# A tuned one-core attention and expert kernel: four of a quartet's sends issued ahead of GpSimd's next inverse deviations

## The reference

```
x = x + attention(layernorm(x), context, mask)     # 16 heads of 8, softmax, output weight Wo
h = layernorm(x)                                   # (v + 1e-5) ** -0.5
probs = softmax(h @ wg.T)                          # 8 experts
topk_w, topk_idx = top_k(probs, 2); topk_w /= sum(topk_w)
y[e] = (silu(h @ w1[e].T) * (h @ w3[e].T)) @ w2[e].T
x = x + sum over the two chosen e of topk_w * y[e]
```

## Time and profile before

| | |
|---|---|
| median of 3 runs | 311.91 us (311.3 to 312.0) |
| profiled execution, its own time | 308.16 us |
| its span | 306.4 us |
| mean granted TensorE clock | 0.893 |
| busy: PE, DVE, ACT, POOL | 75%, 72%, 46%, 37% of the span |
| chain that ended last, by engine | PE 44%, DVE 23%, DMA 14%, SP's queue 8%, issue 7%, ACT 2%, POOL 1% |
| POOL L989, sends | 24, mean 986 ns |
| POOL L972, waiting for DVE's variances (mv, L1059) | 67.6 us in 7 waits |

### The profile page before, as it was taken

The page is one execution under the profiler, slowest core; times in us unless marked ns, Lnnn a source line. Parts: engine busy times, 40 slices in busy tenths (PEclk is TensorE's granted clock), DMA queues, the critical chain, the costliest instruction groups (busy, mean ns, idle before and its releaser), DMA issues.

```text
span 306.4 us, 5812 instructions
## 1 busy us (share of the span) xinstructions
PE 230.8 (75%) x1591; PEld 179.1 (58%) x1591; DVE 219.5 (72%) x642; ACT 142.2 (46%) x318; POOL 114.1 (37%) x125
## 2 busy tenths in 40 slices
PE   0975788999899799695749772979598995999600
PEld 0752565666576566574537551768587994898500
DVE  5578976877578877977482762487788883789853
ACT  5785247554746375250244363435244552555200
POOL 5301250125011251053646343045266776354640
PEclk9996599999999999887586798699889998999955
DMA  6894522442244204427021151402112343254006
GB/s 188 251 275 99 116 49 61 89 99 65 48 101 86 43 19 98 91 63 206 12 52 35 30 111 42 116 9 65 51 51 71 92 111 96 63 137 128 29 21 194
DMA packets 43886, 27.31 MB, mean 89 GB/s; under 512 B 5030, under 2 KB 41397, under 8 KB 43856
## 3 DMA queue, kind: packets, MB, share of 16 engines
q1 hardware_dynamic: 40208, 20.95, 29.4%
q0 software_dynamic: 2816, 5.27, 5.6%
q10 hardware_dynamic: 832, 0.72, 0.9%
HBM read 13.27 MB, written 7.37 MB: 67 GB/s over the span
## 4 chain that ended last, share of the span: by engine, by line
PE 44%; DVE 23%; DMA 14%; SPq 8%; issue 7%; ACT 2%; POOL 1%; POOLq 0%; DVEq 0%
SPq L422 7%; PE bank L495 7%; DVE m_neg L1369 4%; DMA bd<-st 4%; DMA xg<-raw,rows_i 4%; PE bank L501 4%; PE bank L732 4%; PE bank L706 4%; PE bank L709 3%; PE bank L707 3%; PE bank L668 3%; PE bank L629 3%; PE bank L733 3%; PE bank L719 3%; PE bank L651 2%
## 5 line engine op out<-in xcount | busy, mean ns | idle before, releaser
L1028 POOL DMA_INDIRECT ys<-big x46 | 45.1, 981 | 36.0 <-DVE big L1392 14.4
L1369 DVE TENSOR_REDUCE m_neg<-bank 128x4 f32<-128x512 f32 x64 | 43.3, 682 | 15.3 <-PE bank L668 14.9
L909 ACT ACTIVATE big<-bank 128x512 f32<-128x512 f32 x64 | 37.5, 599 | 23.3 <-PE bank L654 22.8
L775 ACT ACTIVATE st<-bank 128x128 fp32r<-128x128 f32 (+1 forms) x92 | 26.3, 329 | 33.5 <-PE bank L719 19.4
L668 PE MATMUL bank<-bd,st 128*128 128x512 f32 x64 | 29.7, 496 | 5.9 <-DMA bd<-st 5.6
L989 POOL DMA_INDIRECT xg<-rows,rows_i x24 | 23.7, 986 | 26.8 <-DVE rows_i L1198 11.9
L651 PE MATMUL bank<-m_bd,ones_b 128*128 128x512 f32 x64 | 31.1, 486 | 2.6 <-ACT big L909 2.2
L1295 DVE SCALAR_TENSOR_TENSOR st<-st_hi,cst,bank 128x512 fp32r<-128x512 f32 x32 | 23.5, 747 | 9.3 <-ACT st_hi L775 4.6
L732 PE MATMUL bank<-bd,st 128*128 x92 | 27.3, 318 | 2.5 <-DVE big L1392 2.1
L941 ACT ACTIVATE big<-bank 128x256 f32<-128x256 f32 x46 | 17.7, 384 | 21.5 <-PE bank L709 20.2
L1411 DVE TENSOR_TENSOR big<-big,bank 128x256 f32<-128x256 f32 x46 | 19.2, 418 | 10.9 <-ACT big L941 10.5
(11 more groups left out here) (172 smaller groups left out, 560.9 us busy)
## 6 DMA issues: line engine op xcount, KB each, us to landing
bd<-st SPq DMA_DIRECT2D x128, 64.0 KB, 2.0
big<-xg SPq DMA_DIRECT2D x46, 64.5 KB, 1.9
raw<-ys SPq DMA_DIRECT2D x8, 256.0 KB, 4.0
xg<-in_patterns SPq DMA_DIRECT2D x18, 64.5 KB
x_all<-in_x SPq DMA_DIRECT2D x4, 256.0 KB, 4.3
rows<-in_mask_BxS_if POOLq DMA_DIRECT2D x4, 256.0 KB, 4.7
ctx_all<-in_L_ffn_w SPq DMA_DIRECT2D x1, 1024.0 KB, 6.4
out<-ctx_all SPq DMA_DIRECT2D x4, 256.0 KB, 3.6
```

What stands on the lines that cost most here:

```text
L775: return nc.scalar.activation(o, i, ACT.Copy)
L909: nc.scalar.activation(prob[n % 2][:, NJ * g:NJ * (g + 1), :].rearrange("p h q -> p (h q)"), s2[k % 2][:, :], ACT.Exp, scale=SCALE).then_i ...
L1028: pool.indirect_dma_start(ys[f], bass.IndirectOffsetOnAxis(xt[n % XR][:, D:RW].bitcast(I32), 0), y_sb[n % YR], None, bounds_check=2 * CAPS ...
L1369: nc.vector.tensor_reduce(m_neg[:, H * (b - 1) + NJ * g:H * (b - 1) + NJ * (g + 1)], s1[k % s1_ring(u)][:, :].rearrange("p (j q) -> p j q" ...
```

## The change

POOL's order alone is changed. The sends of quartet 1 are issued in two halves: batches 4 and 5 (four sends) right after the products of L1006 and ahead of the third quartet's inverse deviations, batches 6 and 7 after these.

```
-            def send_quartet(q):
+            def send_quartet(q, first, last):
                 pool.wait_ge(rows_ready, q + 1)
-                for m in range(2 * QB):
+                for m in range(2 * first, 2 * last):
                     send(QB * q + m // 2, m % 2)
...
                 if u + 1 == NQ:
                     inverse_deviation(NQ)
                     inverse_deviation(NQ + 1)
-                    send_quartet(0)
+                    send_quartet(0, 0, QB)
+            send_quartet(1, 0, 2)
             inverse_deviation(NQ + 2)
-            send_quartet(1)
-            send_quartet(2)
+            send_quartet(1, 2, QB)
+            send_quartet(2, 0, QB)
             inverse_deviation(NQ + 3)
```

## The result

| | before | changed kernel |
|---|---|---|
| median of 20 runs each, us | 311.96 (307.67 to 314.59) | 314.33 (310.31 to 317.67) |
| ratio, 95% interval | | 1.0093 (1.0052 to 1.0133) |
| profiled execution, own time, us | 308.16 | 314.76 |
| its span, us | 306.4 | 313.0 |
| mean granted clock | 0.893 | 0.875 |

The changed kernel is slower, by 0.93% or 2.9 us, with 1.6 to 4.1 us in the interval. The ratio leaves out executions in a slower state of the chip, so it is not the quotient of the two medians, which is 1.0076. Two later measurements of the same kernel, on other occasions, gave 1.0044 (0.9991 to 1.0097) and 1.0039 (1.0004 to 1.0073), 1.4 and 1.2 us. Single executions of one kernel are spread over some 7 us, so the total tells the sign and a size of 1 to 3 us. The mechanism has to be read from intervals inside the traces, which repeat far better.

What follows compares the result with a forecast made beforehand. One unbroken dependent chain, from DVE's third-quartet statistics to the first gathered tile, was taken as the bound. Delaying L1077 by 2.12 us, with nothing saved, gave 311.91 + 2.1 = 314.0 us, range 312.9 to 315.4.

Steps and rivals of the forecast that it cites:

- The sends don't fit into the gap: GpSimd's 3.49 us idle before L972 cannot hold four sends, since the third must wait until the first has landed.
- The sum for the delay: On GpSimd, four sends, then L972 and L973, put L1077 at 160.00 instead of 157.88: 2.12 us later.
- low bound of 1.7: Delay of L1077 in us with the low ends: 3.08 from first to third send, 0.03 for L972 behind a send.
- First send behind the products: On GpSimd, the first moved send starts 0.20 us after the products of L1006, at 152.86.
- first to third send: On GpSimd, 3.30 us, taken between 3.08 and 3.46 seen elsewhere, as no other transfer runs there.
- L972 behind a send: On GpSimd, the step from the fourth send's end to L972, taken as 0.20 us between bounds of 0.03 and 0.31.
- L972 to L973: On GpSimd, 0.31 us between these two instructions that make the inverse deviations.
- The slack of 0.34 us: Before L1077 on DVE, the inverse deviations could end 0.34 us later without delaying it.
- All steps to the first tile shift alike: Behind L1077, quartet 2's sends and SP's padding writes hang on DVE's routing, so the 2.1 us delay finds no cover.
- my first rival: TensorE's clock rises at the same moment though PE restarts later, giving 1.05 us back: +1.1, 313.0 us; chance 0.15.
- The expert stage starts from the gathered tile: In the expert stage every engine starts from the first gathered tile (189.61), so its delay carries through to the end.
- What the edit saves is worth nothing: Quartet 1's second half ends about 4 us sooner, but GpSimd already idled 4.02 us before quartet 2: worth 0.

Runs made afterwards that it cites:

- Warm_after: The changed kernel plus sixteen matmuls whose result nobody reads, on PE ahead of the turn of the third quartet's tokens; ratio 0.9962 to the kernel before.
- eight_ahead: The change with all eight sends of quartet 1, instead of four, ahead of the third quartet's inverse deviations; ratio 1.0258 to the kernel before.
- three_ahead: The change with three sends of quartet 1 instead of four ahead of the inverse deviations; 323.12 us in one execution, beside 323.06 for the kernel before.
- busy_ahead: The kernel before plus five unread powers on GpSimd between the products of L1006 and the inverse deviations, no send moved; ratio 1.0028.

## Why the prediction was right

The forecast was +2.1 us, 314.0 us, slower with 0.87; measured 314.33 us, and a ratio of 1.0093 where 1.0067 was forecast, which lies in all three intervals. The sign and the mechanism up to the token tags are right. That the median came within 0.3 us of the forecast is partly luck: the traces show 1.8 us at the tags but only 0.6 to 1.0 at the row numbers, and later measurements gave 1.4 and 1.2 us. The noise was also taken too small, 0.2%; the intervals reach 0.3 to 0.5% to either side. Step by step:

- **The sends don't fit into the gap.** Right. L972 has no wait for DVE left and starts as soon as the fourth send ends. With two sends the cost is zero, with three 0.55 us, with four 1.77, with eight 8.67.
- **The sum for the delay** was 2.12 us, measured 1.77, near the low bound of 1.7. First send behind the products 0.20, measured 0.16; first to third send 3.30, measured 159.65 - 156.50 = 3.15, so it lay nearer to the undisturbed 3.08 than to the 3.30 that I took; L972 behind a send 0.20, measured 0.02, the step for which there was no row and whose low bound was the right one; L972 to L973 0.31, measured 0.35. The landing for which the third send waits, that of the first, took 2.36 us on the chain. The Trainium skill ("DMA: Bandwidth & Descriptors", "Anatomy of one DMA — SWDGE (gpsimd) path") would have it 2.15 by its formula, an estimate, and the delay at 1.8. That is what came out, but through the 0.02 us and not through the landing, which was 0.21 longer.
- **The slack of 0.34 us** was right: with three sends the inverse deviations end 9.77 us behind the start of the products instead of 8.87, so 0.90 later, and the tags move by 0.55; 0.35 are absorbed.
- **"All steps to the first tile shift alike"** is the step that failed in size. Row numbers came 0.6 to 1.0 us late, not 1.8 or 2.1. Most of that was my first rival, given 0.15, by which the clock rises at the same moment though PE restarts later, and gives half of the shift back. It happened in all three profiled executions: the rise is 17.5, 17.1 and 16.8 us behind the start of the products, in the two of before 17.2 and 17.0. What I held against it, that the wait is longer and not shorter, was no argument, since the low stretch begins within the wait. The other 0.2 us are L1175's, which no rival named. Warm_after shows that nothing else up to the row numbers has slack.
- **"The expert stage starts from the gathered tile"** was right as far as eight_ahead tells: 7.73 us at the gather, 8.0 at the end.
- **What the edit saves is worth nothing.** Right for the sends: quartet 1 is sent 4.35 us sooner, and GpSimd's idle time ahead of quartet 2 grows to 9.26 us. But L1175 on DVE, which no longer meets the last of these sends, is 0.2 us shorter.

The delay less what comes back makes 0.8 us at the row numbers on average (24.89 over three executions of the change, 24.11 over two of before). The first gathers are on average 1.5 us later (42.04 and 40.49), and the totals 1.2 to 2.9 us. That the first measurement is above the two later ones is within their intervals; what it has beyond the 0.8 us is not explained by any run here, and the scatter of quartet 2's sends (15.0 to 16.7 us to the gather) is large enough to hold it.

## What to carry to other kernels

An idle gap on a side engine is room for other work only up to the moment at which the waited-for value arrives; count the moved instructions with their own waits against that gap, and look for who needs the result behind it. Here the gap held two sends and not four, and what was gained by sending early had no taker but for 0.2 us on DVE. Where a small change must be judged under a noise of its own size, make the same change larger (eight sends) and read intervals from a common instruction inside the trace.

## What was not expected of the hardware

- The low clock after PE's restart was shorter after the longer wait: 5.4 to 5.6 us after a wait of 4.2 (the tags-to-logits stretch 8.9 to 9.0 us in three executions), 3.4 to 4.1 after one of 6.0 (8.0 to 8.3 in three). The rows say why: counted from the fall of the clock, which lies within the wait, the low stretch has 6.8 us in each of these six executions, and the same in three_ahead and busy_ahead. In eight_ahead, where PE waits 12.7 us, it is 13.7 us. The Trainium skill, "TensorE: Matmul & The Clock Gate", "What's actually happening", says that the throttled state is the default and activity releases it, which the restart at 0.50 bears out.
- Eight matmuls of 2.1 us in all, put into the wait of 4.2 us, hold the clock at the high level and make the kernel 0.8% faster (ratio 0.9884 to 0.9957). At the start of the expert stage the high clock brings nothing that the runs show.
- More sends under way make the kernel 4% slower, with standstills of 5.3 us on PE, 6.5 on ACT and 7.6 on DVE, engines that issue none of them, and with padding writes on SP that take 9.75 us to issue instead of 5.52.
- A short DVE instruction beside the last send of quartet 1 took 0.39 and 0.37 us, and 0.18 elsewhere.
- A computing instruction on GpSimd starts 0.02 to 0.03 us behind a send; the next send needs 0.30.
